# Attention block on one core: DVE's side work moved ahead of the row maximum, v's products a step earlier

## The chip, the cores and the metric

One core of one Trainium2 chip runs the kernel. The metric is the device time of one execution in microseconds (us). Engines are named as in the profile: PE (TensorE: matmuls and transposes), DVE (VectorE), ACT (ScalarE), POOL (GpSimd), SP (the engine whose queue, SPq, issues DMAs here).

## The reference

Four images of 128 channels and 1024 positions pass through one self-attention block with group normalisation (32 groups of 4 channels) and a residual:

```python
h = (h - mu) * rsqrt(var + EPS) * gamma + beta        # per image and group
q, k, v = w_qkv @ h + b_qkv                           # 3 x [1024, 128]
attn = softmax((q @ k.T) / sqrt(C))                   # [1024, 1024]
out = x + w_proj @ (attn @ v).T + b_proj
```

Inputs and output are float32.

## The kernel before

**What is computed in which form.** q and k are folded into one matrix, so that scores are t·z with t = A z (z is the normalised image), and v is folded with the projection. Every product in half precision is made of a high and a low part: z_hi and z_lo, t_hi and t_lo, v_hi and v_lo, and for the probabilities p_hl[.., 0] and p_hl[.., 1]. Three matmuls (high·high, high·low, low·high) stand for one.

**Steps.** The main loop has 32 steps g, one for each tile of 128 query rows. b = g // 8 is the image and s = g % 8 the step within it. Each engine has its own instruction list, with the order written by hand, and semaphores between them. The memory planning is static: the scores have two slots in PSUM (SLOTS), the probabilities four buffers (RING), their transposes six (PT_RING), and the product with v trails by LAG = 4 steps.

In step g the engines do this:

- **PE** (lines 839 to 887): `score_tile(g)` (six 512-column matmuls, L754 to L756), then `values(g - 4)` (16 matmuls L772/L773 on the high part of the transposed probabilities, 8 matmuls L780 on the low part), then `turn(g - 5)` (a transpose of the result, L793). After that comes side work: `v_products(b, half)` (12 matmuls, L737 to L739) in steps s = 1 and 2, `group_mean` and `group_var` (one-column matmuls for the statistics of image b + 2) in s = 5 and 6, `t_products(b + 1, half)` (L728 to L730) in s = 6 and 7. `values(g)` first waits on `out_ready` at g - 1 (L766): the result of two tiles earlier must have been read out of PSUM by DVE's `add_input(g - 2)`. `score_tile(8b)` waits for `t_low(b, 0)` (L744).
- **DVE** (lines 637 to 680): `scale_output(g - 5)` (L569), `add_input(g - 6)` (L575), `maxima(g)` (the row maximum L550 and the exponent's bias L555), `inverse_sum(g - 1)` (a reciprocal, L560). Behind these stands the side work for this image and the next ones: `t_low` (L538), `v_low` (L545), `channel_stats` (L496 to L501), `group_mean` (L521 to L526) and `group_var` (L531).
- **ACT** (468 to 480): `exponentials(g)` (L435), `p_high(g)` (L442), then `v_high` (L419) in s = 1 and 2 and `t_high` (L414) in s = 6 and 7.
- **POOL** (374 to 396): `p_low(g)`, a subtraction (L344), and for the image after next `power`, `normalise`, `z_high`, `z_low`.
- **SP** (277 to 290): in each step one DMA transpose of the high part (L282, waits for `p_high(g)`) and one of the low part (L286, waits for `p_low(g)`), and every fourth step a store of four tiles (L274). They go out one behind the other in this order.

The last two tiles are handled apart: the high parts of tiles 30 and 31 and the low part of tile 31 are transposed on PE and copied back by DVE and ACT, while the low part of tile 30 still goes through SPq. Its product is the `values(LAST - 1)` near the end of PE's list.

Of the kernel before, what the change touches and what calls it, by code (L numbers as in the profile page):

```python
# [15 lines left out]
B = 4  # L16
# [27 lines left out]
def attention_block(nc, x, gamma, beta, w_qkv, b_qkv, w_proj, b_proj, out):  # L44
# [4 lines left out]
    with ExitStack() as ctx:  # L49
# [159 lines left out]
        tlo_ready = sem("tlo_ready")  # L209
# [36 lines left out]
        def t_part(b, half):  # L246

            return b * 2 + half + 2
# [150 lines left out]
        def _(act):  # L399
# [17 lines left out]
            def v_high(b, half):  # L417
                act.wait_ge(v_psum, b * 2 + half + 1)
                nc.scalar.activation(v_hi[:, b * N + half * HALF:b * N + (half + 1) * HALF], misc[:, half],  # L419
                                     ACT.Copy).then_inc(vhi_ready, 1)  # L420
# [47 lines left out]
            for g in range(G):  # L468
                b, s = divmod(g, TILES)
                exponentials(g)  # L470
                p_high(g)
                if g == 1:
                    v_high(0, 0)
                    v_high(0, 1)
                if s in (1, 2) and b >= 1:
                    v_high(b, s - 1)
                if g in (2, 3):
                    z_high(1, g - 2)
                if s in (6, 7) and b + 1 < B:
                    t_high(b + 1, s - 6)  # L480
# [9 lines left out]
        def _(dve):  # L490
            def channel_stats(b, half):
                if b == 0:
                    dve.wait_ge(x_first[half], 16)
                else:
                    dve.wait_ge(x_rest[b - 1], 16)
                nc.vector.bn_stats(bn[:, b, half, :], x_sb[:, b * N + half * HALF:b * N + (half + 1) * HALF]  # L496
                                   ).then_inc(bn_done, 1)
                if half == 1:
                    dve.wait_ge(bn_done, b * 2 + 2)
                    nc.vector.tensor_copy(bn_seen[:], bn[:, b, half, 0:1])  # L500
                    nc.vector.bn_aggr(chan_mv[:, b], bn[:, b].rearrange("p a f -> p (a f)")).then_inc(chan_ready, 1)  # L501
# [40 lines left out]
            def v_low(b, half):  # L542
                dve.wait_ge(vhi_ready, b * 2 + half + 1)
                cols = slice(b * N + half * HALF, b * N + (half + 1) * HALF)
                nc.vector.tensor_tensor(v_lo[:, cols], misc[:, half], v_hi[:, cols], ALU.subtract  # L545
                                        ).then_inc(vlo_ready, 1)

            def maxima(g):
                dve.wait_ge(scores_ready, g + 1)
                nc.vector.tensor_reduce(row_max[:, g:g + 1], scores[:, g % SLOTS], AX_X, ALU.max  # L550
                                        ).then_inc(max_ready, 1)
                if g >= LAG:
                    dve.wait_ge(max_ready, g + 1)
                    dve.wait_ge(esc_ready, 2)
                    nc.vector.tensor_scalar(exp_bias[:, g:g + 1], row_max[:, g:g + 1], neg_esc[:],  # L555
                                            LOG2_P * math.log(2.0), ALU.mult, ALU.add).then_inc(bias_ready, 1)
# [15 lines left out]
            def add_input(g):  # L572
                dve.wait_ge(turned, g + 1)
                cols = slice(g * P, (g + 1) * P)
                nc.vector.scalar_tensor_tensor(out=out_sb[:, cols], in0=o_ps[:, g % 2, P:2 * P], scalar=bo[:],  # L575
                                               in1=x_sb[:, cols], op0=ALU.add, op1=ALU.add).then_inc(out_ready, 1)
# [60 lines left out]
            for g in range(G):  # L637
                b, s = divmod(g, TILES)
                done = g - LAG - 1
                if done >= 0:  # L640
                    scale_output(done)
                if done >= 1:
                    add_input(done - 1)
                maxima(g)
                if g >= 1:
                    inverse_sum(g - 1)
                if g == 0:
                    t_low(0, 1)
                    dve.wait_ge(wmax_psum, 1)
                    nc.vector.tensor_reduce(w_max[:, 1:2], o_ps[:, 1, 2 * P:3 * P], AX_X, ALU.max).then_inc(wmax_all, 1)  # L650
                    dve.wait_ge(wmax_all, 1)
                    nc.vector.tensor_scalar(w_max[:, 2:3], w_max[:, 1:2], 1.0 / V_MAX, TINY, ALU.mult, ALU.max
                                            ).then_inc(wmax_safe, 1)
                    dve.wait_ge(wmax_safe, 1)
                    nc.vector.reciprocal(w_inv[:], w_max[:, 2:3]).then_inc(winv_ready, 1)
                if g == 1:
                    channel_stats(1, 0)
                    channel_stats(1, 1)
                if g == 2:
                    nc.vector.tensor_copy(ident16[:], ident32[:]).then_inc(ident16_ready, 1)  # L660
                    dve.wait_ge(bo_psum, 1)
                    dve.wait_ge(o_loaded, 32)
                    nc.vector.tensor_tensor(bo[:], bp_c[:], o_ps[:, 0, 0:1], ALU.add).then_inc(bo_ready, 1)
                    group_mean(1)
                    v_low(0, 0)
                    group_var(1)
                    v_low(0, 1)
                if s in (2, 3) and b >= 1:
                    v_low(b, s - 2)
                if b + 2 < B:  # L670
                    if s in (3 if b == 0 else 1, 4):
                        channel_stats(b + 2, s // 4)
                    if s == 5:
                        group_mean(b + 2)
                    if s == 6:
                        group_var(b + 2)
                if s == 7 and b + 1 < B:
                    t_low(b + 1, 0)
                if s == 0 and b >= 1:
                    t_low(b, 1)  # L680


            scale_output(LAST - 4)
# [25 lines left out]
        def _(pe):  # L709
# [129 lines left out]
            for g in range(G):  # L839
                b, s = divmod(g, TILES)  # L840
                score_tile(g)
                if g == 0:
                    t_products(0, 1)
                    pe.wait_ge(wdiag_ready, 1)
                    nc.tensor.matmul(o_ps[:, 1, 2 * P:3 * P], onesb[:], w_diag[:], start=True, stop=True
                                     ).then_inc(wmax_psum, 1)
                if g == 1:
                    pe.wait_ge(wraw_ready, 1)
                    pe.wait_ge(o_loaded, 32)
                    nc.tensor.matmul(o_ps[:, 0, 0:1], w_raw[:], beta_c[:], start=True, stop=False)  # L850
                    nc.tensor.matmul(o_ps[:, 0, 0:1], wpT[:], bv_c[:], start=False, stop=True).then_inc(bo_psum, 1)
                if g >= LAG:
                    if g == LAG + 1:
                        pe.wait_ge(vareps_ready, 2)
                    values(g - LAG)
                if g > LAG:
                    turn(g - LAG - 1)
                if g == 2:
                    pe.wait_ge(w_ready, 1)
                    for half in range(2):  # L860
                        pe.wait_ge(tlo_ready, t_part(0, half))
                        v_products(0, half)
                if s in (1, 2) and b >= 1:
                    pe.wait_ge(tlo_ready, t_part(b, s - 1))
                    v_products(b, s - 1)

                if g == 3:
                    group_mean(1)
                    pe.wait_ge(bo_ready, 1)
                    for _ in range(KEEP_WARM):  # L870
                        nc.tensor.matmul(o_ps[:, 0, 0:HALF], ones16[:], warm[:], start=True, stop=True)
                    group_var(1)

                if s == 5 and b + 2 < B:
                    pe.wait_ge(vlo_ready, b * 2 + 1)
                    group_mean(b + 2)
                if s == 6 and b + 2 < B:
                    pe.wait_ge(vlo_ready, b * 2 + 2)
                    group_var(b + 2)
                if s == 6 and b + 1 < B:  # L880
                    pe.wait_ge(mean_ready, min(b + 3, B))
                    pe.wait_ge(vlo_ready, b * 2 + 1)
                    t_products(b + 1, 0)
                if s == 7 and b + 1 < B:
                    pe.wait_ge(vareps_ready, min(b + 3, B))
                    pe.wait_ge(vlo_ready, b * 2 + 2)
                    t_products(b + 1, 1)
# [43 lines left out]
```

## Time and profile before

| | |
|---|---|
| time, median of 3 runs | 128.53 us (128.05 to 128.63) |
| time of the profiled execution | 128.79 us |
| its span in the trace | 126.9 us |
| PE busy | 115.3 us (91%) |
| DVE / ACT / POOL busy | 94.1 / 91.8 / 87.3 us |
| SP's DMA queue q1 | 88.9% of 16 engines' span |
| start of step 8, 16, 24 (PE) | 38.92, 65.12, 90.70 us |
| start of step 31 (PE) | 111.88 us |

The span runs from the first to the last instruction; the execution's own time has 1.9 us around it. PE's matmuls are pipelined: a 512-column one is shown with 0.38 us but the next starts 0.22 us later, and a 128-column one with 0.22 us at a distance of 0.06 us. So a stall of PE is read from distances between starts, not from the idle column alone.

### The profile page before, as it was taken

The page shows a single profiled execution, that of the slowest core. Times are in us where ns is not written, and L with a number is a line of the kernel's source. Part 1 is how long each engine was busy: PE and PEld are TensorE (multiplying, and loading weights), DVE is VectorE, ACT ScalarE, POOL GpSimd, SP SyncE. Part 2 cuts the span into 40 slices and gives each one's busy share as a digit, 9 for nine tenths or more (in the row PEclk, how much of TensorE's full clock was granted, in tenths as well). Part 3 has the DMA queues.
Part 4 walks back from the last instruction along what each step waited for, and adds up shares of the span by engine and source line. Part 5 has one row for each costly group of instructions (what it writes and reads, how often), then busy time and mean ns, then how long its engine had stood idle before and what let it go on. Part 6 is the DMA issues. An engine that isn't in the chain of part 4 may idle for free.

```text
span 126.9 us, 3214 instructions
## 1 busy us (share of the span) xinstructions
PE 115.3 (91%) x1187; PEld 79.3 (62%) x1187; DVE 94.1 (74%) x237; ACT 91.8 (72%) x130; POOL 87.3 (69%) x73
## 2 busy tenths in 40 slices
PE   5976979689999999999999999999999999998981
PEld 2351346357675677667656786776568867777970
DVE  3687389788866967998569588775796887776832
ACT  3026279999989787887877878878878788788200
POOL 2054119888999998999758997999666665766000
PEclk9995599999999999999999999999999999999999
DMA  2584003699999999999999999999999999999602
GB/s 88 161 327 169 0 0 67 127 110 209 188 97 168 196 184 124 222 222 185 195 184 201 187 106 291 195 140 204 213 173 120 213 229 138 205 188 229 166 5 83
DMA packets 67727, 20.66 MB, mean 163 GB/s; under 512 B 65408, under 2 KB 66176, under 8 KB 67712
## 3 DMA queue, kind: packets, MB, share of 16 engines
q1 hardware_dynamic: 67280, 20.46, 88.9%
q8 instruction: 9, 0.15, 0.5%
q10 hardware_dynamic: 432, 0.00, 0.2%
q14 instruction: 6, 0.05, 0.1%
HBM read 2.36 MB, written 2.10 MB: 35 GB/s over the span
## 4 chain that ended last, share of the span: by engine, by line
PE 69%; ACT 10%; DVE 7%; DMA 7%; issue 3%; POOL 1%; SPq 0%; POOLq 0%
PE scores L754 11%; PE o_ps L772 10%; PE scores L756 10%; PE scores L755 10%; PE o_ps L780 9%; PE o_ps L773 9%; ACT probs L435 4%; DMA ptT<-p_hl 4%; DMA x_sb<-in_x_dram 3%; DVE row_max L550 3%; ACT p_hl L442 2%; PE o_ps L793 2%; DVE t_lo L538 2%; ACT z_hi L408 1%; PE misc L728 1%
## 5 line engine op out<-in xcount | busy, mean ns | idle before, releaser
L344 POOL TENSOR_TENSOR p_hl<-probs,p_hl 128x1024 f16<-128x1024 f32 x31 | 66.0, 2132 | 14.5 <-ACT p_hl L442 14.3
L550 DVE TENSOR_REDUCE row_max<-scores 128x1 f32<-128x1024 f32 x32 | 39.1, 1222 | 18.3 <-PE scores L756 18.2
L435 ACT ACTIVATE probs<-scores,exp_bias,esc 128x1024 f32<-128x1024 f32 x32 | 38.5, 1202 | 14.3 <-DVE exp_bias L555 14.2
L442 ACT ACTIVATE p_hl<-probs 128x1024 f16<-128x1024 f32 x32 | 33.8, 1057 | 1.0
L772 PE MATMUL o_ps<-v_hi,ptT 128*128 128x128 f16 x256 | 32.0, 219 | 1.7 <-issue 1.3
L773 PE MATMUL o_ps<-v_lo,ptT 128*128 128x128 f16 x256 | 32.0, 219 | 0.0
L772 PEld LDWEIGHTS o_ps<-v_hi,ptT 128*128 128x128 f16 x256 | 24.9, 98 | 8.2 <-issue 5.9
L754 PE MATMUL scores<-z_hi,t_hi 128*128 128x512 f16 x64 | 24.8, 387 | 2.9 <-ACT probs L435 2.4
L773 PEld LDWEIGHTS o_ps<-v_lo,ptT 128*128 128x128 f16 x256 | 25.0, 98 | 2.3
L755 PE MATMUL scores<-z_lo,t_hi 128*128 128x512 f16 x64 | 24.8, 387 | 0.0
L756 PE MATMUL scores<-z_hi,t_lo 128*128 128x512 f16 x64 | 24.8, 387 | 0.0
L780 PE MATMUL o_ps<-v_hi,ptT 128*128 128x128 f16 x256 | 19.5, 219 | 0.4 <-DMA ptT<-p_hl 0.4
L780 PEld LDWEIGHTS o_ps<-v_hi,ptT 128*128 128x128 f16 x256 | 15.6, 98 | 0.6 <-DMA ptT<-p_hl 0.6
L569 DVE TENSOR_SCALAR oT_sb<-o_ps,rinv,w_out 128x128 f32<-128x128 f32 x32 | 12.8, 400 | 2.5 <-PE o_ps L780 2.0
L754 PEld LDWEIGHTS scores<-z_hi,t_hi 128*128 128x128 f16 x64 | 6.5, 101 | 9.7 <-issue 2.9
L575 DVE SCALAR_TENSOR_TENSOR out_sb<-o_ps,bo,x_sb 128x128 f32<-128x128 f32 x32 | 11.0, 343 | 1.3 <-PE o_ps L793 1.3
L756 PEld LDWEIGHTS scores<-z_hi,t_lo 128*128 128x128 f16 x64 | 6.3, 99 | 7.9 <-issue 0.6
L793 PE MATMUL o_ps<-ident,oT_sb 128*128 128x128 f32 x32 | 9.0, 281 | 0.4 <-DVE oT_sb L569 0.4
L755 PEld LDWEIGHTS scores<-z_lo,t_hi 128*128 128x128 f16 x64 | 6.3, 99 | 4.4 <-issue 0.3
L414 ACT ACTIVATE t_hi<-misc,ct 128x512 f16<-128x512 f32 (+1 forms) x8 | 5.3, 660 | 3.2 <-PE misc L730 3.2
L337 POOL TENSOR_TENSOR z_lo<-z,z_hi 128x512 f16<-128x512 f32 x6 | 7.0, 1160 | 0.0
L798 PE MATMUL scores<-warm,ones 128*128 128x512 f16 x12 | 5.6, 610 | 1.4 <-DVE warm L506 1.4
(136 smaller groups left out, 140.2 us busy)
## 6 DMA issues: line engine op xcount, KB each, us to landing
out_dram<-out_sb SPq DMA_DIRECT2D x7, 256.0 KB, 2.6
x_sb<-in_x_dram SPq DMA_DIRECT2D x3, 512.0 KB, 4.8
ptT<-p_hl SPq DMA_TRANSPOSE x61, 3.5
x_sb<-in_x_dram SPq DMA_DIRECT2D x2, 256.0 KB, 3.3
out_dram<-out_sb SPq DMA_DIRECT2D x1, 192.0 KB, 2.0
wqkv_sb<-in_L_conv_w_qkv_dram SPq DMA_DIRECT2D x1, 128.0 KB, 3.8
wp_sb<-in_L_conv_w_proj_dram SPq DMA_DIRECT2D x1, 64.0 KB, 3.5
wqkv_sb<-in_L_conv_w_qkv_dram SPq DMA_DIRECT2D x1, 64.0 KB, 3.2
```

Source lines behind the costliest of these rows:

```text
L344: nc.gpsimd.tensor_tensor(p_hl[:, g % RING, 1], probs[:, g % RING], p_hl[:, g % RING, 0], ALU.subtract).then_inc(plo_ready, 1)
L435: nc.scalar.activation(probs[:, g % RING], scores[:, g % SLOTS], ACT.Exp, bias=exp_bias[:, g:g + 1], scale=esc[:], accum_out=row_sum[:, g: ...
L442: nc.scalar.activation(p_hl[:, g % RING, 0], probs[:, g % RING], ACT.Copy).then_inc(phi_ready, 1)
L550: nc.vector.tensor_reduce(row_max[:, g:g + 1], scores[:, g % SLOTS], AX_X, ALU.max).then_inc(max_ready, 1)
L569: nc.vector.tensor_scalar(oT_sb[:, g % 2], o_ps[:, g % 2, 0:P], rinv[:, g:g + 1], w_out[:], ALU.mult, ALU.mult).then_inc(oT_ready, 1)
L754: nc.tensor.matmul(dst, t_hi[:, rows], z_hi[:, cols], start=True, stop=False)
L755: nc.tensor.matmul(dst, t_hi[:, rows], z_lo[:, cols], start=False, stop=False)
L756: last = nc.tensor.matmul(dst, t_lo[:, rows], z_hi[:, cols], start=False, stop=True)
L772: nc.tensor.matmul(dst, hi, v_hi[:, keys], start=(k == 0), stop=False)
L773: nc.tensor.matmul(dst, hi, v_lo[:, keys], start=False, stop=False)
L780: last = nc.tensor.matmul(dst, ptT[:, g % PT_RING, 1, k], v_hi[:, keys], start=False, stop=(k == TILES - 1))
L793: nc.tensor.transpose(o_ps[:, g % 2, P:2 * P], oT_sb[:, g % 2], ident32[:]).then_inc(turned, 1)
```

## The change

Three lists are edited. On DVE, the side work of images 1 to 3 moves from behind the reciprocal to the place between `add_input` and `maxima`. Some of it also changes its step: `t_low(b, 1)` goes from s = 0 to s = 1, `channel_stats(3, ..)` from s = 1 and 4 to s = 4 and 5, `group_mean` from s = 5 to 6, `group_var` from s = 6 to 7. `t_low(b + 1, 0)` stays behind `maxima` but goes ahead of the reciprocal. `channel_stats(2, ..)` stays where it was. On PE, `v_products(b, half)` goes from s = 1 and 2 to s = 0 and 1, for images 1 to 3, and on ACT `v_high(b, half)` with it.

```diff
--- before.py
+++ after.py
@@ -472,8 +472,8 @@
                 if g == 1:
                     v_high(0, 0)
                     v_high(0, 1)
-                if s in (1, 2) and b >= 1:
-                    v_high(b, s - 1)
+                if s in (0, 1) and b >= 1:
+                    v_high(b, s)
                 if g in (2, 3):
                     z_high(1, g - 2)
                 if s in (6, 7) and b + 1 < B:
@@ -641,7 +641,20 @@
                     scale_output(done)
                 if done >= 1:
                     add_input(done - 1)
+
+                if s == 1 and b >= 1:
+                    t_low(b, 1)
+                if s in (2, 3) and b >= 1:
+                    v_low(b, s - 2)
+                if s in (4, 5) and 1 <= b < B - 2:
+                    channel_stats(b + 2, s - 4)
+                if s == 6 and b + 2 < B:
+                    group_mean(b + 2)
+                if s == 7 and b + 2 < B:
+                    group_var(b + 2)
                 maxima(g)
+                if s == 7 and b + 1 < B:
+                    t_low(b + 1, 0)
                 if g >= 1:
                     inverse_sum(g - 1)
                 if g == 0:
@@ -665,19 +678,8 @@
                     v_low(0, 0)
                     group_var(1)
                     v_low(0, 1)
-                if s in (2, 3) and b >= 1:
-                    v_low(b, s - 2)
-                if b + 2 < B:
-                    if s in (3 if b == 0 else 1, 4):
-                        channel_stats(b + 2, s // 4)
-                    if s == 5:
-                        group_mean(b + 2)
-                    if s == 6:
-                        group_var(b + 2)
-                if s == 7 and b + 1 < B:
-                    t_low(b + 1, 0)
-                if s == 0 and b >= 1:
-                    t_low(b, 1)
+                if g in (3, 4):
+                    channel_stats(2, g - 3)
 
 
             scale_output(LAST - 4)
@@ -860,9 +862,9 @@
                     for half in range(2):
                         pe.wait_ge(tlo_ready, t_part(0, half))
                         v_products(0, half)
-                if s in (1, 2) and b >= 1:
-                    pe.wait_ge(tlo_ready, t_part(b, s - 1))
-                    v_products(b, s - 1)
+                if s in (0, 1) and b >= 1:
+                    pe.wait_ge(tlo_ready, t_part(b, s))
+                    v_products(b, s)
 
                 if g == 3:
                     group_mean(1)
```

## Rows read from the trace of the kernel before

**Rows 1.** Page: busy time, share of the span and instructions of each engine.
```profile
PE 115.3 (91%) x1187; PEld 79.3 (62%) x1187; DVE 94.1 (74%) x237; ACT 91.8 (72%) x130; POOL 87.3 (69%) x73
```

**Rows 2.** Timeline (start us, us, engine, line), step 29, without side work.
```profile
106.38 0.38 PE L754 MATMUL scores<-z_hi,t_hi 128*128 128x512 f16 x1
107.67 0.22 PE L772 MATMUL o_ps<-v_hi,ptT 128*128 128x128 f16 x1
...
109.13 0.38 PE L754 MATMUL scores<-z_hi,t_hi 128*128 128x512 f16 x1
...
109.64 0.34 DVE L575 SCALAR_TENSOR_TENSOR out_sb<-o_ps,bo,x_sb 128x128 f32<-128x128 f32 x1
...
110.62 1.23 DVE L550 TENSOR_REDUCE row_max<-scores 128x1 f32<-128x1024 f32 x1 [0.64 <-PE scores L756]
```

**Rows 3.** Timeline, step 9, up to the start of step 10.
```profile
41.68 0.38 PE L754 MATMUL scores<-z_hi,t_hi 128*128 128x512 f16 x1
...
41.89 0.73 DVE L538 SCALAR_TENSOR_TENSOR t_lo<-misc,ct,t_hi 128x512 f16<-128x512 f32 x1
...
42.86 0.34 DVE L575 SCALAR_TENSOR_TENSOR out_sb<-o_ps,bo,x_sb 128x128 f32<-128x128 f32 x1
...
43.30 0.22 PE L772 MATMUL o_ps<-v_hi,ptT 128*128 128x128 f16 x1 [0.16 <-issue]
...
45.42 0.38 PE L754 MATMUL scores<-z_hi,t_hi 128*128 128x512 f16 x1
```

**Rows 4.** Timeline, step 12: start of the step and of values.
```profile
51.59 0.38 PE L754 MATMUL scores<-z_hi,t_hi 128*128 128x512 f16 x1
...
53.15 0.22 PE L772 MATMUL o_ps<-v_hi,ptT 128*128 128x128 f16 x1
```

**Rows 5.** Timeline, image boundary: end of step 7, start of step 8.
```profile
38.06 0.15 DVE L560 RECIPROCAL rinv<-row_sum 128x1 f32<-128x1 f32 x1
38.13 0.73 DVE L538 SCALAR_TENSOR_TENSOR t_lo<-misc,ct,t_hi 128x512 f16<-128x512 f32 x1
...
38.36 0.38 PE L730 MATMUL misc<-z_hi,a_lo 128*128 128x512 f16 x1
...
38.92 0.39 PE L754 MATMUL scores<-z_hi,t_hi 128*128 128x512 f16 x1 [0.18 <-DVE t_lo L538]
```

**Rows 6.** Group of v_low's instructions by form: count, busy us, mean ns.
```profile
L545 DVE TENSOR_TENSOR v_lo<-misc,v_hi 128x512 f16<-128x512 f32 x8 | 5.4, 674 | 0.0
```

**Rows 7.** Timeline of SPq: transposes of high (L282), low (L286), a store.
```profile
60.21 1.34 SPq L286 DMA_TRANSPOSE ptT<-p_hl  x1
...
62.98 1.98 SPq L286 DMA_TRANSPOSE ptT<-p_hl  x1
...
80.74 1.26 SPq L282 DMA_TRANSPOSE ptT<-p_hl  x1
82.67 1.23 SPq L286 DMA_TRANSPOSE ptT<-p_hl  x1
...
91.95 1.32 SPq L286 DMA_TRANSPOSE ptT<-p_hl  x1
93.78 1.23 SPq L282 DMA_TRANSPOSE ptT<-p_hl  x1
...
115.39 0.58 SPq L274 DMA_DIRECT2D out_dram<-out_sb  x1
116.80 1.23 SPq L286 DMA_TRANSPOSE ptT<-p_hl  x1
```

**Rows 8.** Timeline of POOL: low parts of tiles 18, 21 and 30.
```profile
77.09 2.14 POOL L344 TENSOR_TENSOR p_hl<-probs,p_hl 128x1024 f16<-128x1024 f32 x1 [0.95 <-ACT p_hl L442]
...
86.47 2.14 POOL L344 TENSOR_TENSOR p_hl<-probs,p_hl 128x1024 f16<-128x1024 f32 x1
...
114.59 2.13 POOL L344 TENSOR_TENSOR p_hl<-probs,p_hl 128x1024 f16<-128x1024 f32 x1 [0.62 <-ACT p_hl L442]
```

**Rows 9.** Timeline of PE near the end: it waits for tile 30's transpose.
```profile
121.61 0.56 PE L780 MATMUL o_ps<-v_hi,ptT 128*128 128x128 f16 x7 [0.39 <-DMA ptT<-p_hl]
```

## The prediction

> **What bounds the kernel now.** I read the page first. PE is busy for 91% of the span [rows 1], so what can be won there is what it idles. The summary of waits hides part of that, because a pipelined matmul is shown longer than its distance to the next. So I read the timeline of PE and measured the distances between starts.
>
> A step without side work takes 2.75 us (106.38 to 109.13), and its values begin 1.29 us after its scores [rows 2]. In step 9 they begin 1.62 us after (41.68 to 43.30), 0.33 us later than that. DVE's addition starts at 42.86 and takes 0.34 us, so it ends at 43.20, and PE goes on 0.10 us later [rows 3]. This is the wait on `out_ready` at L766. The addition is late because t_low(1, 1) stood ahead of it (from 41.89, for 0.73 us). In step 12 it is 1.56 us instead of 1.29 [rows 4], behind v_low(1, 1) of step 11. The same table of starts gives eight such places: steps 9, 17, 25 (t_low of step s = 0; 0.32 us each above the 1.30 of other side-work steps), steps 12, 20, 28 (v_low; 0.26 each), step 13 (channel_stats; 0.26) and step 14 (group_mean; 0.08). Rows 3 and 4 show one of each of the two large kinds.
>
> At an image's start PE waits for t_low(b, 0). Its last matmul of step 7 starts at 38.36 and the next could follow at 38.58, but follows at 38.92: 0.34 us [rows 5]. This comes three times (steps 8, 16, 24).
>
> The second view is SP's queue. A pair of transposes takes 2.77 us there when one is issued behind the other (60.21 to 62.98) [rows 7]. That is as long as PE's plain step of 2.75 [rows 2], and the queue also has a store every fourth step (0.58 us long) [rows 7] and now and then a slow issue, of 1.98 us instead of 1.34 [rows 7]. So the queue is a second bound close behind PE: in the trace it has hardly a rest from 37 to 73 us. After that it rests only where it waits for POOL: 0.67 us ahead of 82.67 (80.74 + 1.26 to 82.67) and 0.8 us ahead of 116.80 (115.39 + 0.58 to 116.80) [rows 7], and, for no reason shown, 0.5 us ahead of 93.78 (91.95 + 1.30 to 93.78) [rows 7].
>
> The third view is the chain that ended last, read backwards. It ends through the low part of tile 30: POOL ends it at 114.59 + 2.13 = 116.72 [rows 8], the queue issues it at 116.80 [rows 7], and PE takes it up at 121.61 after a short wait [rows 9]. Whatever is won in the loop reaches the end only as far as this transpose is issued earlier.
>
> **The change, part by part.** *DVE's work ahead of the maximum.* In a plain step the addition starts at 109.64, ends at 109.98, and the maximum starts at 110.62: 0.64 us are free [rows 2]. v_low takes 0.67 [rows 6], and channel_stats' first part much the same. Since DVE's operations overlap by some 0.07 us at their ends (38.06 + 0.15 against 38.13, rows 5), the effective price is about 0.6, and the step is just filled. t_low is 0.73 [rows 3], but step 9 follows a longer step 8, so there is room. Only channel_stats' second half, which has two small operations behind it, is longer (some 0.9 us), and puts one maximum 0.2 us late (step 13); exp of that step is needed two steps later, so it costs nothing. What goes away is the late addition: 3 x 0.32 + 3 x 0.26 + 0.26 + 0.08 = 2.08 us of PE time. Next late in these steps is nothing on DVE: the addition would have to slip by 0.4 us more to be felt. Bounds: 2.08 if all fits, 1.5 if every full step passes 0.1 us on.
>
> *t_low(b + 1, 0) ahead of the reciprocal.* The reciprocal takes 0.07 us of the chain at the boundary (38.06 to 38.13) [rows 5]: 3 x 0.07 = 0.21 us. The remaining 0.27 of each stall stays, since the maximum itself is still in front. The reciprocal is wanted five steps later and is free.
>
> *group_mean and group_var one step later.* Their results are awaited by PE behind values and turn of the same step, over 1 us after DVE has them, and by POOL behind its subtraction. No cost; if that cover were gone, at most 0.4 us.
>
> *v's products one step sooner.* Twelve matmuls per half. Step 9 lasts 3.74 us (41.68 to 45.42) [rows 3], less 2.75 and the 0.32 stall it leaves 0.67 for them. They move by a step, six times, and are not removed: sum zero. Step 9, 17 and 25 therefore start some 0.6 us later than they would, and ACT's and POOL's work of these tiles too; two steps on this is made good. ACT's v_high moves along, behind p_high, where ACT waits for the next bias anyway: free.
>
> PE's sum is 2.08 + 0.21 = 2.29 us earlier at step 31; 0.2 us of it is gone again in the pieces I can't see, or not: bounds 1.7 to 2.3.
>
> *What the queue lets through.* PE's gain at the start of step 18 is that of steps 8, 9, 12, 13, 14, 16 and 17, less the 0.67 of the half of v's products that now lies ahead of it: 0.07 + 0.32 + 0.26 + 0.26 + 0.08 + 0.07 + 0.32 - 0.67 = 0.71. POOL works without a rest from tile 18's subtraction (77.09) to tile 21's (86.47, ending at 88.60) [rows 8]. So tile 21's low transpose moves by those 0.71 us and no more; the queue, which wins 0.6 us of rest ahead of 82.67, nearly keeps up. From there to the end of the store at 115.97 the queue goes without a rest but the 0.5 ahead of 93.78 [rows 7], so the store also ends 0.7 earlier, at 115.25. POOL would have tile 30 ready at 116.72 - 2.29 = 114.43. The queue is later, so the last transpose goes out at about 115.25 + 0.08 = 115.33 instead of 116.80: a gain of **1.47 us**. Bounds: 2.29 (POOL sets it; the queue is quicker) and 0.83 (one more slow issue, 0.64 longer, falls into the full stretch). I take 1.47, from the rows nearest to it. It is then taken 4.8 us later, as now (116.80 to 121.61) [rows 7, 9].
>
> A rule of the Trainium skill speaks against this limit. "DMA: Bandwidth & Descriptors", section "Latency and other measured facts", gives 261 GB/s for a DMA transpose. By it one transpose of 262,144 bytes would take an estimated 1.0 us and a pair 2.0, and the queue would never bound. The trace disagrees with 2.77 us for the pair, which is 189 GB/s, and I go by the trace.
>
> **The sum.** 128.79 (the profiled execution) - 1.47 = 127.3. That execution was 0.26 us above the median of 128.53; from the median it is 127.06. I forecast 127.1.
>
> **The rivals.**
> 1. *The queue follows and PE's whole gain arrives.* The slow issues in the queue come from nothing that the trace names, and the 0.5 us ahead of 93.78 may close. Then the last transpose goes out when POOL is ready: 128.53 - 2.3 = **126.2**. For it: the queue did rest 0.8 us before the last issue. Against: it has no rest in 27 us before that.
> 2. *The queue eats most of it.* It is kept full for longer, and one or two more slow issues (0.64 us each) fall into the stretch that now has nothing to spare: 1.47 - 0.64 = 0.83 or 1.47 - 1.28 = 0.19, so **127.7 to 128.3**. For it: slow issues come every 7 to 10 instructions. Against: they might go by the instruction count, which stays.
> 3. *The change doesn't take the stall away.* If DVE is full from s = 2 to 5 (price 0.6 in a gap of 0.64), a little more per operation makes each addition as late as before, and only the t_low places (3 x 0.32) and 0.21 stay: 1.2 at PE, some 0.6 at the end: **127.9**.
> 4. *Slower.* The queue again: with transposes always waiting, slow issues come three times as often in the last 28 us, say four more at 0.64 = 2.56 us. From the third additional one on (1.92 > 1.47) the last transpose is later than now: 128.53 - 1.47 + 2.56 = **129.6**.
>
> **How the numbers follow.** Forecast 0.42 (its own range 126.7 to 127.6), rival 1 0.25, rival 2 0.16, rival 3 0.11, rival 4 0.06. A measurement of this kernel tells 0.5%, 0.64 us, from no change, so faster means under 127.9: all of the forecast and of rival 1 and half of rivals 2 and 3, 0.80; same 0.14; slower 0.06. The range of 126.1 to 128.2 takes in the forecast, rival 1 and most of 2 and 3; it leaves out rival 4 and what is beyond the bounds.
>
> **What would show it.** In the changed kernel's timeline: the values of steps 9, 12, 13, 17, 20, 25 and 28 start 1.30 us after their scores; maxima start 1.5 us after the step's start, except that of step 13; PE's first matmul of steps 8, 16 and 24 still waits for t_low, by 0.27; step 8 takes 3.4 us and step 10 2.75; step 31 starts near 109.6. If the queue binds, it goes from about 88 us to the last transpose with no rest over 0.1 us but the one near 93, the last low transpose goes out by itself within 0.1 us of the store before it, and POOL's subtraction of tile 30 is done 0.5 to 0.9 us before it is issued. If that issue follows POOL instead, rival 1 holds. The prediction is wrong if values begin late again (rival 3), or if SPq's issues of 2 us become more than the eight or so of now (rivals 2 and 4).

## The result and the profile after

| | before | changed |
|---|---|---|
| median of 20 runs | 128.53 us (128.02 to 129.28) | 128.53 us (126.77 to 130.57) |
| ratio to before | | 0.994, 95% interval 0.991 to 0.997 |
| later runs of both, on one chip | 128.93 us (23 runs) | 128.95 us (12 runs, 126.23 to 129.63); ratio 0.986, 0.981 to 0.990 |
| profiled execution: time, span | 128.79, 126.9 us | 129.85, 128.1 us |
| start of step 5, of step 31 on PE | 28.66, 111.88 us | 28.40, 110.24 us |

The ratio compares only runs within 1.5% of the fastest of each kernel; the changed kernel's runs spread over 3.8 us, so this leaves out 9 of the 20, and the median of all 20 says no gain at all. Both belong to the result: 0.6% faster by the ratio, nothing by the median, and three times as wide a spread.

The profiled execution of the changed kernel is one of its longer ones. It still shows each step of the change. The page's first row, against [rows 1]:

```profile
PE 115.7 (90%) x1187; PEld 81.4 (64%) x1187; DVE 93.3 (73%) x237; ACT 91.9 (72%) x130; POOL 87.2 (68%) x73
```

The timeline of the changed kernel in steps 8 to 12 (start us, us, engine, line), against [rows 2 to 5]. L756 is the first matmul of the scores here, L774 the first of values, L782 values' third product:

```profile
37.79 0.74 DVE L538 SCALAR_TENSOR_TENSOR t_lo<-misc,ct,t_hi 128x512 f16<-128x512 f32 x1
38.45 0.15 DVE L560 RECIPROCAL rinv<-row_sum 128x1 f32<-128x1 f32 x1
38.59 0.39 PE L756 MATMUL scores<-z_hi,t_hi 128*128 128x512 f16 x1
...
41.87 0.34 DVE L575 SCALAR_TENSOR_TENSOR out_sb<-o_ps,bo,x_sb 128x128 f32<-128x128 f32 x1
42.02 0.38 PE L756 MATMUL scores<-z_hi,t_hi 128*128 128x512 f16 x1
42.12 0.74 DVE L538 SCALAR_TENSOR_TENSOR t_lo<-misc,ct,t_hi 128x512 f16<-128x512 f32 x1
43.32 0.22 PE L774 MATMUL o_ps<-v_hi,ptT 128*128 128x128 f16 x1
43.52 1.23 DVE L550 TENSOR_REDUCE row_max<-scores 128x1 f32<-128x1024 f32 x1 [0.65 <-PE scores L758]
...
50.95 0.38 PE L756 MATMUL scores<-z_hi,t_hi 128*128 128x512 f16 x1
51.46 0.34 DVE L575 SCALAR_TENSOR_TENSOR out_sb<-o_ps,bo,x_sb 128x128 f32<-128x128 f32 x1
51.72 0.68 DVE L496 BATCH_NORM_STATS2 bn<-x_sb 128x6 f32<-128x512 f32 x1
52.24 0.22 PE L774 MATMUL o_ps<-v_hi,ptT 128*128 128x128 f16 x1
52.44 1.23 DVE L550 TENSOR_REDUCE row_max<-scores 128x1 f32<-128x1024 f32 x1
```

Values of step 9 begin 1.30 us after the scores (42.02 to 43.32) instead of 1.62, those of step 12 1.29 (50.95 to 52.24) instead of 1.56. The side work stands between addition and maximum, and the maximum still starts 1.5 us after the step. t_lo goes ahead of the reciprocal. All eight late additions are gone.

The other half of the picture is the queue and the end. The timeline of SPq in the changed kernel, its POOL row for tile 30 and PE's row that waits, against [rows 7 to 9]:

```profile
112.39 1.29 SPq L282 DMA_TRANSPOSE ptT<-p_hl  x1
113.72 1.35 SPq L286 DMA_TRANSPOSE ptT<-p_hl  x1
115.12 2.04 SPq L274 DMA_DIRECT2D out_dram<-out_sb  x1
117.25 1.28 SPq L286 DMA_TRANSPOSE ptT<-p_hl  x1
...
112.96 2.14 POOL L344 TENSOR_TENSOR p_hl<-probs,p_hl 128x1024 f16<-128x1024 f32 x1 [1.32 <-ACT p_hl L442]
...
117.80 0.29 PE L774 MATMUL o_ps<-v_hi,ptT 128*128 128x128 f16 x1 [2.12 <-DMA ptT<-p_hl]
```

POOL has tile 30's low part at 115.10, 1.62 us earlier than before, but the queue issues it at 117.25, 0.45 us later than before. And PE now waits 2.12 us for tile 29's high part, for which it did not wait before. A view of the DMA engines from 114 to 118 us shows why. "DMA" is their busy share in tenths in 40 slices of 0.1 us, and q8 is the queue on which instructions are fetched:

```profile
DMA  9999429999989999999000000000010000079999
q8 instruction: 1, 0.02, 2.6%
```

For some 1.5 us, from about 115.9, hardly a packet moves, with transposes waiting. One fetch of 16 KB, begun at 115.1, reaches into this stretch. The page counts nine such fetches in either kernel.

The wait has a second cost. After it PE runs at half its clock. The view of windows gives the times of a stretch, then each engine's busy us with the number of its instructions (PE, PEld, DVE, ACT, POOL), then PE's granted clock, the DMA engines' share and GB/s. First the changed kernel as profiled here, from the end of PE's wait, then a second profile of the same kernel (after_again below), also from the end of its wait for tile 29, which is 1.78 us there:

```profile
117.80:121.10 3.30, 3.30 (x31) 3.24 (x32) 0.52 (x2) 0.00 (x0) 0.00 (x0) 0.50 0.93 255
```

```profile
117.60:120.90 3.30, 3.30 (x57) 3.28 (x58) 1.53 (x5) 1.02 (x1) 0.00 (x0) 1.00 0.91 252
```

In the first PE gets through 31 matmuls in 3.3 us, in the second through 57. A granted clock of 0.50 is the lower of its two levels (1.2 GHz instead of 2.4). From the end of this wait to the first values of tile 30 PE needs 4.05 us (117.80 to 121.85) instead of 2.47 (117.59 to 120.06). So the halved clock costs 1.6 us of this execution.

The mean granted clock is on record for each of these runs, profiled or not. It is 0.96 in 7 of the 20 runs of the changed kernel, and 0.97 to 1.00 in the other 13. A stretch of 3.4 us at half clock, as in this trace, takes 1.7 of 128 us, 0.013 of the mean: the step from 0.973 to 0.960. The 7 have a median of 129.85 us, the 13 one of 128.18. That the 7 all had their half-clock stretch at this place is an inference from this one trace. Two of the 13 took 130.0 us without it, which stays unexplained.

### The profile page after: what moved, and what is told of

Same layout as the page of the kernel before. It is cut to its first block, busy times and chain, and to the rows that moved or that the text cites. A ratio compares the mean times of both kernels' runs of the same rounds, so it can differ in the third digit from the quotient of the medians.

```text
span 128.1 us, 3214 instructions
## 1 busy us (share of the span) xinstructions
PE 115.7 (90%) x1187; PEld 81.4 (64%) x1187; DVE 93.3 (73%) x237; ACT 91.9 (72%) x130; POOL 87.2 (68%) x73
## 4 chain that ended last, share of the span: by engine, by line
PE 66%; DMA 11%; ACT 10%; DVE 7%; issue 2%; POOL 1%; SPq 0%; POOLq 0%
PE scores L756 10%; PE o_ps L782 9%; PE scores L758 9%; PE o_ps L774 9%; PE scores L757 9%; PE o_ps L775 9%; DMA ptT<-p_hl 8%; ACT probs L435 4%; DMA x_sb<-in_x_dram 3%; DVE row_max L550 3%; ACT p_hl L442 2%; PE o_ps L795 2%; DVE t_lo L538 2%; ACT z_hi L408 1%; PE misc L741 1%
## 5 line engine op out<-in xcount | busy, mean ns | idle before, releaser
L550 DVE TENSOR_REDUCE row_max<-scores 128x1 f32<-128x1024 f32 x32 | 39.0, 1220 | 18.0 <-PE scores L758 17.9
L774 PE MATMUL o_ps<-v_hi,ptT 128*128 128x128 f16 x256 | 32.8, 222 | 2.4 <-DMA ptT<-p_hl 2.1
L775 PE MATMUL o_ps<-v_lo,ptT 128*128 128x128 f16 x256 | 32.8, 222 | 0.0
L774 PEld LDWEIGHTS o_ps<-v_hi,ptT 128*128 128x128 f16 x256 | 25.4, 99 | 6.1 <-DMA ptT<-p_hl 2.3
L756 PE MATMUL scores<-z_hi,t_hi 128*128 128x512 f16 x64 | 24.7, 387 | 2.9 <-ACT probs L435 2.6
L782 PE MATMUL o_ps<-v_hi,ptT 128*128 128x128 f16 x256 | 20.0, 222 | 0.5 <-DMA ptT<-p_hl 0.5
L782 PEld LDWEIGHTS o_ps<-v_hi,ptT 128*128 128x128 f16 x256 | 15.9, 99 | 1.0 <-DMA ptT<-p_hl 0.9
L756 PEld LDWEIGHTS scores<-z_hi,t_hi 128*128 128x128 f16 x64 | 6.5, 101 | 9.7 <-issue 3.1
L555 DVE TENSOR_SCALAR exp_bias<-row_max,neg_esc 128x1 f32<-128x1 f32 x28 | 6.0, 214 | 1.0
## 6 DMA issues: line engine op xcount, KB each, us to landing
wqkv_sb<-in_L_conv_w_qkv_dram SPq DMA_DIRECT2D x1, 128.0 KB, 3.9
```

What stands on the lines that cost most here:

```text
L756: nc.tensor.matmul(dst, t_hi[:, rows], z_hi[:, cols], start=True, stop=False)
L774: nc.tensor.matmul(dst, hi, v_hi[:, keys], start=(k == 0), stop=False)
L775: nc.tensor.matmul(dst, hi, v_lo[:, keys], start=False, stop=False)
L782: last = nc.tensor.matmul(dst, ptT[:, g % PT_RING, 1, k], v_hi[:, keys], start=False, stop=(k == TILES - 1))
```

## The experiments

Two theories. **Q**: the DMA queue of the transposes is full and takes PE's gain. **P**: it isn't the queue; the gain is lost on PE, DVE or POOL. A third, **F**, came with the view above: a fetch of instructions stops the transposes for over a us, and where the last one falls decides over the end. after_again is the changed kernel itself, run once more.

| kernel | median us (runs) | lowest to highest | runs with the extra half-clock stretch | step 5 to 31 on PE | last transpose after step 5 | step 31 to end |
|---|---|---|---|---|---|---|
| before | 128.53 (20) | 128.0 to 129.3 | 0 of 86 later ones | 83.22 | 88.14 | 15.0 |
| changed | 128.53 (20) | 126.8 to 130.6 | 7 | 81.84 | 88.85 | 17.9 |
| after_again | 128.95 (12) | 126.2 to 129.6 | 6 | 81.09 | 87.76 | 16.0 |
| b_nolow | 127.95 (12) | 127.4 to 128.8 | 0 | 83.21 | none | 14.4 |
| a_nolow | 126.26 (6) | 125.1 to 126.5 | 0 | 80.97 | none | 14.4 |
| v_only | 128.06 (12) | 127.5 to 129.0 | 0 | 82.52 | 87.45 | 15.2 |
| dve_only | 137.10 (6) | 136.5 to 137.2 | 6 | 91.12 | 96.04 | 15.1 |
| b_actstore | 129.00 (12) | 128.1 to 129.6 | 0 | 83.22 | 88.16 | 15.1 |
| a_actstore | 129.94 (7) | 127.7 to 131.0 | 5 | 82.29 | 87.54 | 15.0 |
| b_shift54 | 128.53 (12) | 127.8 to 130.0 | 1 | 83.22 | 88.37 | 14.5 |
| b_shift126 | 128.05 (12) | 127.6 to 128.8 | 0 | 83.21 | 88.13 | 14.5 |
| a_shift54 | 126.92 (6) | 126.1 to 128.0 | 0 | 81.25 | 87.87 | 15.8 |
| a_shift126 | 127.16 (6) | 126.9 to 127.8 | 0 | 80.97 | 87.88 | 16.0 |
| a_shift258 | 128.48 (12) | 126.5 to 130.8 | 4 | 80.96 | 87.75 | 16.1 |

Before itself had medians of 128.53 to 128.93 us beside these. The extra stretch is read from a run's mean granted clock: 0.962 or less, or 0.987, where the others of the same kernel have 0.968 to 0.973, or 0.995 and more. The last three columns are differences of times in the one profiled execution of each, the last to the end of its span, to 0.1 us.

The start of step 5 itself lies between 28.3 and 29.4 us in these traces, whatever the kernel. It goes with the same clock. In the seven traces with a mean of 0.973 or less it lies at 28.27 to 28.93 (the early head). There PE's 512-column matmuls go over from a distance of 0.43 us to 0.22 between 14.9 and 16.6 us. In the seven with 0.997 or more it lies at 29.05 to 29.39 (the late head), and they go over at 16.7 to 17.4 us. So a run tells by its mean clock which of the two heads it had. "After step 5" leaves the head out.

**The queue relieved.** Both kernels without the low parts' transposes. The third product of values reads the high part instead, so the result is not the attention's. The waits of POOL, DVE and PE for these transposes go too:

```diff
-                if g < LAST:
-                    sp.wait_ge(plo_ready, g + 1)
-                    sp.dma_start(ptT[:, g % PT_RING, 1], p_hl[:, g % RING, 1], transpose=True
-                                 ).then_inc(lo_transposed[g % RING], 16)
...
-                    last = nc.tensor.matmul(dst, ptT[:, g % PT_RING, 1, k], v_hi[:, keys], start=False,
+                    last = nc.tensor.matmul(dst, ptT[:, g % PT_RING, 1 if g == LAST else 0, k], v_hi[:, keys], start=False,
```

> The kernel before without the 31 DMA transposes of the low parts (L286); the third product of values takes the high part's transpose instead, so that PE's and POOL's work stay as they are and the output is not the attention's. It is the base for a_nolow. Theory Q (the DMA queue of the transposes is full and sets the end): the kernel before was bound by PE, the queue second, so it gains only the wait for tile 30's low transpose, 0.5 us: about 128.0. Theory P (the queue is not what ate the gain): the same number.

> The changed kernel with the same edit: no DMA transposes of the low parts, the third product takes the high part. Theory Q: with half the transposes the queue is no bound, and PE's whole gain of 2.3 us arrives: 128.0 - 2.3 = 125.7, 1.8% under b_nolow, and runs lie close together. Theory P: the difference stays what it is between the full kernels, 0.6% (0.8 us): about 127.2, and the spread between runs stays as wide (126.8 to 130.6).

b_nolow took 127.95 us and a_nolow 126.26: with the queue relieved the change is worth 1.7 us, 1.3%, where it is worth 0.6% or nothing with it. The page of a_nolow shows the queue at half of the 88.9% of the kernel before (packets, MB, share):

```profile
q1 hardware_dynamic: 34544, 12.33, 45.4%
```

PE's starts of steps 5 and 31, first of b_nolow and then of a_nolow, show the loop:

```profile
28.57 0.38 PE L748 MATMUL scores<-z_hi,t_hi 128*128 128x512 f16 x1 [0.61 <-ACT probs L430]
...
111.78 0.38 PE L748 MATMUL scores<-z_hi,t_hi 128*128 128x512 f16 x1
```

```profile
29.29 0.38 PE L750 MATMUL scores<-z_hi,t_hi 128*128 128x512 f16 x1 [0.61 <-ACT probs L430]
...
110.26 0.38 PE L750 MATMUL scores<-z_hi,t_hi 128*128 128x512 f16 x1
```

83.21 against 80.97 us: 2.24 of the 2.29 us forecast for PE, and from step 31 to the end both need 14.4. The medians show 1.7 because four of a_nolow's six runs had the late head and only four of b_nolow's twelve. Among runs with the late head the difference is 2.3 us (128.60 to 126.29, 4 runs each), among those with the early one 2.7 (127.88 to 125.14, 8 and 2 runs). So PE's whole gain arrives when the queue is relieved. With the full queue, step 5 to the end takes 98.2 us before and 97.1 in after_again (step 5 to 31 plus step 31 to the end), 1.1 to 1.2 us less: the queue takes about 1 us of the 2.2. Theory Q holds for this part, and P falls. It does not explain the runs with the halved clock.

**One part alone.** v_only is the kernel before with only PE's and ACT's edits, dve_only the changed kernel without them.

```diff
-                if s in (1, 2) and b >= 1:
-                    pe.wait_ge(tlo_ready, t_part(b, s - 1))
-                    v_products(b, s - 1)
+                if s in (0, 1) and b >= 1:
+                    pe.wait_ge(tlo_ready, t_part(b, s))
+                    v_products(b, s)
```

> The kernel before with v's products and v_high one step sooner and DVE's order as before. Neither theory gives it a gain: the eight late additions stay, as t_low and v_low stand where they stood. 128.5, within 0.3% of before, and values still begin 1.56 to 1.62 us after the scores in steps 9, 12, 13, 17, 20, 25 and 28. If it gained over 0.5 us, the gain of the change would be v's and not DVE's.

I was wrong: 128.06 us, a ratio of 0.995 (0.992 to 0.998). The timeline of v_only in steps 9 and 11:

```profile
41.96 0.38 PE L754 MATMUL scores<-z_hi,t_hi 128*128 128x512 f16 x1
43.25 0.22 PE L772 MATMUL o_ps<-v_hi,ptT 128*128 128x128 f16 x1
...
48.13 0.38 PE L754 MATMUL scores<-z_hi,t_hi 128*128 128x512 f16 x1
49.69 0.22 PE L772 MATMUL o_ps<-v_hi,ptT 128*128 128x128 f16 x1
```

Step 9 has no stall (1.29): as v's products lengthen step 8 by 0.67 us, DVE's addition behind t_low is in time for step 9. The stall of step 12 has moved to step 11 (1.56). The loop is 0.70 us shorter. So a third of PE's gain is had by moving PE's side work under DVE's, with DVE's order untouched.

> The changed kernel with v's products and v_high put back to steps s = 1 and 2; DVE's order stays changed. Now v_low of s = 2 and 3 stands ahead of the maximum but its v_high ends only about 2.1 us after the step's start, where DVE would be free at 0.9. If the move of v's products is needed for the other, the maxima of steps 10, 11, 18, 19, 26 and 27 are late by about 1.3 us each, POOL and the queue get these tiles later; PE itself feels it only if exp is over 2 us late. Theory Q: the end is set by the queue, so 0 to 1 us slower than the changed kernel: 128 to 129.5. Theory P: PE's gain is kept or lost with the maxima alone: 127 to 128.

It took 137.10 us, ratio 1.064, far beyond what I expected. DVE and PE of dve_only around step 12:

```profile
47.79 0.69 DVE L545 TENSOR_TENSOR v_lo<-misc,v_hi 128x512 f16<-128x512 f32 x1 [2.30 <-ACT v_hi L419]
48.40 1.22 DVE L550 TENSOR_REDUCE row_max<-scores 128x1 f32<-128x1024 f32 x1
...
52.80 0.69 DVE L545 TENSOR_TENSOR v_lo<-misc,v_hi 128x512 f16<-128x512 f32 x1 [2.30 <-ACT v_hi L419]
...
55.61 0.22 PE L774 MATMUL o_ps<-v_hi,ptT 128*128 128x128 f16 x1 [2.10 <-DVE out_sb L575]
```

DVE waits 2.30 us for v_hi with the maximum queued behind. The late maximum delays ACT's exp, and ACT's next v_high stands behind that exp, so the next v_low is later still, and then PE waits 2.10 us for an addition. I had priced the first wait (1.3 us) and not the loop through ACT. PE's wait comes in steps 12, 20 and 28. After the one in step 20, and after no other in this trace, PE's clock is halved for 3.4 us (84.7 to 88.1). Steps 20 and 21 take 9.43 us (80.10 to 89.53), steps 28 and 29 with the same work 7.76 (109.54 to 117.30), so this costs 1.7 us of the 8.4. The mean clock says that each of the six runs had one such stretch. The two parts are not a sum: against the 128.72 us of before in these runs they make -0.7 and +8.4 us alone, and 0 to -0.8 together.

**What in the queue is full.** The loop's six stores go out on ACT's queue, after p_high:

```diff
+                done = g - LAG - CT - 2
+                if done >= 0 and done % CT == 0:
+                    act.wait_ge(out_ready, done + CT)
+                    act.dma_start(out_d[done // TILES, :, done % TILES * P:(done % TILES + CT) * P],
+                                  out_sb[:, done * P:(done + CT) * P]).then_inc(stored, 16)
```

> The kernel before with the six stores of the loop issued by ACT, on its own DMA queue, one step later; the transposes keep SP's queue alone. The same bytes pass the same DMA engines. Theory Q1 (what is full is SP's issuing: 0.68 us for a store and the gap behind it, 6 times): the last low transpose is bound by POOL already in this kernel, so about 128.4. Theory Q2 (what is full are the DMA engines and their rings): the same. It is the base for a_actstore.

> The changed kernel with the same edit. Theory Q1 (SP's issuing is full): 6 x 0.68 = 4.1 us of issuing go, the queue rests again, POOL sets the last transpose, 126.3, and the spread narrows. Theory Q2 (the DMA engines are full): nothing is won, 127.5 to 128.5. Theory F (a fetch of instructions, 16 KB on another queue, stops the transposes for about a us, and where it falls near the end decides): 126.3 to 128, with a spread as wide as that of the changed kernel.

b_actstore took 129.00 us (ratio 1.001, interval 0.999 to 1.004), a_actstore 129.94 (7 runs, 127.7 to 131.0; ratio 1.014). None of the three theories had that much for a_actstore. 4.1 us of SP's issuing are gone, and nothing is won. From tile 4's low transpose to tile 30's the queue needs 80.38 us in a_actstore and 80.61 in after_again, so SP's time to issue is not what is full. What lies behind it is, the DMA engines or their rings; the runs don't tell these two apart. The us that the changed kernel lost this way isn't in its trace, which is of its shortest run (127.74 us; 97.3 us from step 5 to the end). Five of the seven runs have the extra half-clock stretch, 129.4 to 131.0 us; the two without it took 127.74 and 129.94. Why the stretch is more frequent here stays open; in the trace the transposes took up to 6.2 us to land.

**Where the fetch falls.** PE gets more instructions ahead of the loop, with the same number of columns, so that the fetches come earlier in the loop:

```diff
-            def warm_up(count):
+            def warm_up(count, pieces=1):
...
+                    for k in range(pieces):
+                        part = slice(k * HALF // pieces, (k + 1) * HALF // pieces)
+                        nc.tensor.matmul(scores[:, 1, part], ones16[:], warm[:, part], start=True, stop=True)
```

with 4 pieces (54 instructions more), 8 (126), and up to 16 together with cut keep-warm matmuls (258).

> The changed kernel with 9 of the warm-up matmuls cut into four of 128 columns each: the same columns, 27 matmuls and 27 weight loads more on PE ahead of the loop. The trace of the changed kernel shows nine fetches of 16 KB on the instruction queue, some 240 to 260 PE instructions apart, each with a stretch in which no transpose moves; the last fell at 115.1 us, onto tile 29's transposes. Theory F: 54 instructions earlier by count is 54/256 x 11.1 us = 2.3 us earlier at each fetch, so the last falls before tile 29's transposes: 2.1 us of waiting near the end go, 126.5. Theory Q: the queue is full wherever the fetches fall, no change against the changed kernel: 127.8 to 128.5.

> The kernel before with the same 54 more PE instructions. In its trace the last fetch fell at 119.6 us, onto tile 30's low transpose (4.8 us to landing instead of 3.4). Theory F: it falls some 2.3 us earlier, ahead of that transpose or onto tile 29's: between 127.6 and 129, moved by over 0.5%. Theory Q: 128.5, no change.

> The changed kernel as it is, as the base for a_shift126 on the same chip. Its 20 runs had a median of 128.53 and lay between 126.8 and 130.6. Both theories: 128.5, with a spread of over 2 us.

> The changed kernel with 9 of the warm-up matmuls cut into eight of 64 columns each: the same columns, 63 matmuls and 63 weight loads more on PE ahead of the loop. The last two fetches of the changed kernel were at 104.2 and 115.1 us; with 54 more instructions they were at 102.1, 112.3 and 122.2. Theory F (where the fetch falls near the end decides): 126 more instructions put them at about 109.5 and 120, ahead of tile 29's high transpose and behind the landing of tile 30's low one: PE waits under 0.7 us for transposes after step 31, and the time is 126.2 to 126.8, that is under a_shift54's 126.9. Theory Q (a full queue alone, wherever the fetches fall): the same as after_again, 128.5. If it is a_shift54's gain by chance, it is between the two.

> The kernel before with the same 126 more PE instructions. Its last fetch fell at 119.6 us onto tile 30's low transpose, whose landing took 4.8 us instead of 3.4, and PE waited 0.4 us for it. Theory F: the last fetches at about 109 and 120, where PE has slack of its own: 128.0 to 128.5, at most 0.5 us under before. Theory Q: 128.5.

> The changed kernel with the warm-up and keep-warm matmuls cut into still more pieces of the same columns, 129 matmuls and 129 weight loads more than in the changed kernel, most of them ahead of the loop. That is one whole distance between two fetches (some 256 PE instructions), so by theory F the fetches near the end fall where they fall in the changed kernel itself, near 104 and 115 us, later by what the head grows (48-odd more small matmuls, 0 to 2.5 us): PE waits about 2 us for tile 29's high transpose again, and from the start of step 31 to the end of the span it is 16 to 18 us instead of a_shift126's 16.0 or less and with a wide spread. If instead the many small matmuls as such were what made a_shift54 and a_shift126 steady, this kernel keeps their 15.8 to 16.0 us from step 31 to the end and PE waits under 0.7 us there.

Measured: a_shift54 126.92, a_shift126 127.16 (ratio to before 0.988, 0.985 to 0.992), after_again 128.95, a_shift258 128.48; b_shift54 128.53 (0.998) and b_shift126 128.05 (0.994). Two of theory F's numbers missed: a_shift126 was to be under a_shift54 and under 126.8, and b_shift54 was to move by over 0.5% and did not move. The DMA engines of a_shift126 from 107 to 111 us, then from 114 to 118 us:

```profile
DMA  9996589999999999946899999990000000000008
q8 instruction: 1, 0.02, 1.7%
```

```profile
DMA  8999999999998589999999999999799997999999
q1 hardware_dynamic: 2771, 0.91, 106.9%
```

The standstill has moved, together with the fetch, from 116 to 110 us, and the last transposes run undisturbed. In a_shift258, one whole distance further, both are back. The same 114 to 118 us, and PE's wait for tile 29:

```profile
DMA  9999919939999999999998000000000000999999
q8 instruction: 1, 0.02, 1.9%
```

```profile
117.71 0.23 PE L774 MATMUL o_ps<-v_hi,ptT 128*128 128x128 f16 x1 [1.85 <-DMA ptT<-p_hl]
```

That the standstill goes with the fetch is shown in the traces, and where it falls is set by the count of PE's instructions. In a_shift126 each of the eight fetches from 30 to 110 us is followed, 0.4 to 0.6 us later, by 1.1 to 1.4 us with hardly a packet.

What it does to the time is shown less directly. From step 31 to the end after_again needs 16.0 us with the standstill on tile 29, a_shift126 the same 16.0 without it, and a_shift258 16.1. In a_shift126 PE waits for the full queue in smaller pieces instead (0.48, 0.65, 0.63 and 0.16 us). So in these traces the standstill by itself makes the end no later. The 0.95 us between the starts of their fifth steps are the two heads.

The difference lies in the runs with the extra half-clock stretch. With the fetch at its old place near the end (changed, after_again, a_shift258) 17 of 44 runs have it; with the shifts of 54 and 126 it is 0 of 12. after_again's six with it have a median of 129.38 us, its six without it 127.18, which is a_shift126's 127.16. So on that chip the long runs carry the whole difference of the medians. The chain is: a fetch near the end, a transpose of tile 29 that lands 1.4 to 2.0 us late, a wait of PE of about 2 us, and after it, in some executions only, half the clock for 3.4 us. The last step is seen in one trace of the changed kernel (wait of 2.12 us) and not in the traces with waits of 1.78 and 1.85. What decides between them isn't shown.

By the medians a_shift126 is 1.8 us under the changed kernel and as much under before, on one chip. By the ratios to before it is level with the changed kernel (0.988 and 0.986): what it removes is the long runs. The same shift also takes 0.9 us off the kernel before, where PE no longer waits for tile 30. With both shifted, the change is worth 0.9 us (128.05 to 127.16).

## Why the prediction was right or wrong

- *PE's part* was right: 2.24 us measured in a_nolow against the kernel without the change, 2.29 worked out. Step 31 starts 81.84 us after step 5 in the changed kernel instead of 83.22, with 0.87 us of new waits for transposes in it (steps 22 and 29), and 81.09 in after_again. The step before each boundary became 0.05 to 0.07 us shorter, for the 0.07 forecast.
- *DVE's free 0.64 us* was right: the maxima keep their 1.50 us, but for step 13 with 1.67 (53.70 to 55.37), the 0.2 us forecast.
- *v's products "sum zero"* was wrong as a price of that part alone: v_only gained 0.70 us in the loop. I had charged the t_low stalls to DVE's order only. It did not hurt the sum, as both edits cure the same three stalls.
- *What the queue lets through*, the 1.47 us of the sum, is the step that failed in its size. The bound itself was right: POOL's tile 30 waits 2.15 us for the queue in the changed kernel. But I forecast 1.47 us for the last transpose. From step 5 on it moved by 0.38 us in after_again (88.14 to 87.76) and by -0.71 in the first profiled execution. I had taken the rests that the queue showed before, 0.67 us and 0.83 us, as time that it could give up. From tile 4's low transpose to tile 30's the queue needs 80.99 us before, 80.61 in after_again and 81.70 in the profiled changed kernel. Issues slower than usual add up to 4.4 us before, and rests to 2.7; afterwards it is 5.5 or 6.7 us of slow issues and 0.5 of rests. The queue took the rests away and paid for them in slow issues. Rival 2 had this for the last transpose (0.19 or 0.83 us). My sign for it, more than eight issues of 2 us, was a poor one: transposes issued in over 1.5 us are 6 before (from 28 us on) and 7 in the first profile after, with one store.
- *The landing of 4.8 us "as now"* was wrong: it is 3.3 us after the change, since the standstill falls three issues earlier, onto tile 29. With it the path to the end changed. PE no longer waits for tile 30's low part, on which the whole sum rested, but for tile 29's high part: the 2.12 us at 117.80. I had seen slow stretches every 7 to 10 issues and called them nameless; the page's row of the instruction queue names what goes with them.
- *The clock* stands in no term of the sum and in no rival. It costs 1.6 us in the profiled execution. Rival 4, slower at 129.6 by four more slow issues, comes near the long runs' 129.85 by its number, not by its mechanism.

From step 5 to the end the kernel before takes 98.2 us, after_again 97.1 and the first profile 99.7. So without the halved clock 1.1 to 1.2 of the 1.47 us arrive. That they come so near is luck: the last transpose moved by 0.38 instead of 1.47, and its landing became 1.4 us shorter instead of staying, so that the end no longer hung on it. Between the two profiles of the changed kernel lie 2.6 us: 1.6 of clock, 0.75 of waits in steps 22 and 29, and 0.3 of a longer wait for tile 29.

The median of 128.53 is 1.4 us above the 127.1 forecast. The 13 runs without the extra half-clock stretch have 128.18. In after_again the six without it have 127.18, at the forecast. Why the two batches differ by 1 us there stays open.

The Trainium skill, "Runtime: NRT & Kernel Launch", section "Instruction fetch mechanics", says that instructions are fetched in blocks of 16 KiB on a DMA queue of their own, 256 instructions each, and that crossing a block's boundary is mostly hidden. The traces agree on 16 KB and on a distance of some 256 PE instructions (207 to 308 in the changed kernel, 255 on the mean), and no row names a wait of PE for instructions. But the cost isn't hidden from the transposes on the full queue, which stood still for about a us each time.

## What to carry to other kernels

When a change frees the busiest engine by a per cent or two, look for the resource that is within as much of its own limit, and don't count its short rests as reserve until a run has used them. To test it, take that resource's load away in both kernels and see whether the gain appears. Work put ahead of an instruction on the critical path needs its inputs earlier as well: without v's move the same order on DVE cost 8.4 us. And when a kernel's runs spread, sort them by their granted clock before looking for a cause: here it separates the long runs of the changed kernel, and the two heads of every kernel.

## What the runs showed of the hardware

- After a wait of 2.12 us for a transpose PE's granted clock was 0.50 for 3.4 us, and PE got through 31 matmuls where it otherwise does 57. After waits of 1.78 and 1.85 us it stayed at 1.00. In dve_only it was halved after one of three waits of 2.10 us.
- With each fetch of 16 KB on the instruction queue, nine times in 100 us, the DMA transposes stood still for some 1 to 1.5 us and landed in up to 5.5 us instead of 3.3. The fetches moved with the number of PE instructions ahead of them.
- SP's queue kept to 80.3 to 81.7 us for the same transposes and stores, whether a producer was 0.1 or 2 us ahead, and six stores moved to another queue did not shorten the kernel (129.0 and 129.9 us).
- PE's loop repeats to 0.01 us between executions (83.21 or 83.22 us in five kernels with the old DVE order and v's products in their old place), while the start of step 5 varies by 1.1 us, with the granted clock of the head.
